# Two segments to a scan, states joined by hand, C products two ring slots back, halos on ScalarE

## The reference, cut to what matters

```python
u, gate = jnp.split(hidden_states @ W_in.T, 2, axis=-1)
u = silu(conv1d_causal(u, conv_w, taps=4) + conv_b)      # per channel
dt, Bm, Cm = split(u @ Wx.T);  dt, Bm, Cm = rmsnorm of each
delta = softplus(dt @ Wdt.T + dt_bias)                     # [L, D]
def step(state, xs):                                       # state [D, N]
    d_t, B_t, C_t, u_t = xs
    dA = jnp.exp(d_t[..., None] * A)
    state = dA * state + (d_t * u_t)[..., None] * B_t[:, None, :]
    return (state, jnp.einsum('bdn,bn->bd', state, C_t))
y = ys + u * D_param
return (y * silu(gate)) @ W_out.T
```

## Time and profile before

| what | us |
|---|---|
| median of 3 runs (1938.14 to 1943.71) | 1939.92 |
| the profiled execution | 1951.26 |
| its span | 1949.5 |
| VectorE busy in the span | 1376.4 |
| TensorE, matmuls | 1617.0 |
| ScalarE | 1094.3 |
| GpSimd | 1008.4 |

### The profile page before, as it was taken

How to read it: one execution, slowest core, us unless ns; L and a number is a source line. 1 busy time by engine, 2 the same in 40 slices (tenths; PEclk the granted TensorE clock), 3 DMA queues, 4 the chain that set the end, 5 groups by cost and what they waited for, 6 DMA issues and landing times. The chain is left out here.

```text
span 1949.5 us, 24260 instructions
## 1 busy us (share of the span) xinstructions
PE 1617.0 (83%) x8168; PEld 865.8 (44%) x8168; DVE 1376.4 (71%) x2292; ACT 1094.3 (56%) x2026; POOL 1008.4 (52%) x598
## 2 busy tenths in 40 slices
PE   6888999999779995788788797887978879745668
PEld 2522222222157443555365474654746547422322
DVE  3258888888073215038998899989999888999423
ACT  2334666667721113257766767668676676765127
POOL 0000000001033103447999899998999989999403
PEclk9866999999965796788698796997969879756678
DMA  5311000000083447543544455444554444545022
GB/s 225 154 52 56 3 3 3 3 3 3 7 297 145 149 129 262 185 107 76 117 103 99 105 123 114 103 98 106 122 115 103 99 104 110 118 98 123 19 91 87
DMA packets 152988, 195.78 MB, mean 100 GB/s; under 512 B 17907, under 2 KB 123139, under 8 KB 151198
## 3 DMA queue, kind: packets, MB, share of 16 engines
q1 hardware_dynamic: 143692, 167.19, 33.0%
q0 software_dynamic: 4608, 16.80, 2.4%
q10 hardware_dynamic: 4564, 10.24, 1.4%
HBM read 141.81 MB, written 52.37 MB: 100 GB/s over the span
## 5 line engine op out<-in xcount | busy, mean ns | idle before, releaser
L1810 DVE TENSOR_TENSOR_SCAN ssm_scan<-ssm_psum,ssm_state,ssm_scan 128x256 f32<-128x256 f32 x1024 | 680.2, 729 | 62.4 <-ACT ssm_psum L1697 61.2
L1429 POOL TENSOR_TENSOR ssm_scan<-ssm_scan,ssm_bc 128x1024 f32<-128x1024 f32 x256 | 554.1, 2176 | 78.3 <-DVE ssm_scan L1810 77.1
L1697 ACT ACTIVATE ssm_psum<-ssm_rep,ssm_a 128x256 f32<-128x256 f32 x1024 | 435.4, 468 | 190.6 <-DVE ssm_scan L1810 188.7
L641 ACT ACTIVATE att_probs<-att_psum 128x1024 f32<-128x1024 f32 x256 | 248.3, 1021 | 104.6 <-PE att_psum L577 104.3
L1409 POOL TENSOR_TENSOR ssm_scan<-ssm_rep,ssm_bc 128x1024 f32<-128x1024 f32 x128 | 301.5, 2356 | 9.2 <-DMA ssm_rep<-drive_rows 9.2
L678 DVE TENSOR_REDUCE att_rowmax<-att_psum 128x1 f32<-128x512 f32 x448 | 277.9, 682 | 38.1 <-PE att_psum L559 37.9
L1533 PE MATMUL ssm_psum<-ssm_scan,ssm_select 128*32 128x256 f32 x2048 | 192.3, 462 | 103.6 <-POOL ssm_scan L1429 103.3
L530 POOL COPY att_v<-v_tokens 128x128 f32<-128x128 f32 x8 | 2.3, 292 | 328.1 <-ACT att_out L635 328.1
L559 PE MATMUL att_psum<-att_k,att_q 72*128 72x512 bf16 x448 | 159.2, 395 | 3.7 <-DVE att_rowmax L678 2.2
L1795 DVE TENSOR_TENSOR ssm_scan<-ssm_rep,ssm_psum 128x1024 f32<-128x1024 f32 x128 | 156.2, 1220 | 1.1 <-DMA ssm_rep<-drive_rows 1.1
L1511 PE MATMUL ssm_psum<-ssm_h,late_weights 128*128 128x256 f32 x512 | 135.4, 424 | 18.2 <-DVE ssm_delta L1784 15.1
(11 more groups left out here) (232 smaller groups left out, 1892.2 us busy)
## 6 DMA issues: line engine op xcount, KB each, us to landing
ssm_rep<-drive_rows SPq DMA_DIRECT2D x256, 256.0 KB, 4.7
qkv_wmod<-in_wmod SPq DMA_DIRECT2D x8, 1536.0 KB, 11.9
late_weights<-in_we SPq DMA_DIRECT2D x8, 1024.0 KB, 14.3
ssm_bc<-bc_rows SPq DMA_DIRECT2D x32, 256.0 KB, 5.1
drive_rows<-ssm_delta SPq DMA_DIRECT2D x64, 128.0 KB
drive_rows<-ssm_du SPq DMA_DIRECT2D x64, 128.0 KB
sorted_rows<-moe_zeros SPq DMA_DIRECT2D x1, 5888.0 KB, 18.9
moe_sorted<-sorted_rows SPq DMA_DIRECT2D x23, 256.0 KB, 3.4
```

The source lines that it names most:

```text
L641: nc.scalar.activation(probs[:, u % RING, :].rearrange("p (j t) -> p j t", j=2), ps_s[u % 2], ACT.Exp).then_inc(exp_done, 1)
L1429: nc.gpsimd.tensor_tensor(read[:, Q % RING], drive[:, Q % RING], bc[:, c % 2, 1, gr, :].unsqueeze(1).to_broadcast([P, J, SW]), ALU.mult).t ...
L1697: nc.scalar.activation(ps_decay[n % HALF_BANKS][:, i], rep[:, s % 2, 0, j, :], ACT.Exp, scale=amat[:, t, gr, j:j + 1]).then_inc(decay_done, 1)
L1810: nc.vector.tensor_tensor_scan(drive[:, Q % RING, j, :], ps_decay[(2 * Q + j // 2) % HALF_BANKS][:, j % 2], drive[:, Q % RING, j, :], stat ...
```

## The change

A scan now covers two segments, 512 columns, with one instruction. The decay of the second segment's first column is set to zero once (`cut`, the decays of an odd segment then leave out their first column), so that the scan starts anew there. What the initial value did is done by hand: the first column's decay exp(A * delta) is computed for the tile (`first_decays`, two TENSOR_SCALARs of four columns on VectorE, and one Exp of eight columns on ScalarE), and `join` adds state times first decay to the first column of the drive for j = 1 and 3, two TENSOR_SCALARs of one column for each unit from chunk 1 on. Rows of the ring are 256 columns, dense; the product with C goes to the slot of two units before, so a spread waits for a sum two units closer; `bc` starts two columns later in memory. The halo copies go from VectorE to ScalarE, ahead of the copy of u. TensorE's and ScalarE's tables change: rows, square, the fourth output product and copy, Silu, the gate copies and the modulation of h move by one or two units.

```diff
+    PHASE = 2
-        halo = sb("ssm_halo", [P, DT, TAPS - 1])
+        halo = sb("ssm_halo", [P, 2, DT, TAPS - 1])
-        bc = sb("ssm_bc", [P, 2, 2, GROUPS, SW])
+        bc = sb("ssm_bc", [P, 2 * 2 * GROUPS * SW + PHASE])[:, PHASE:].rearrange("p (b s g t) -> p b s g t", b=2, s=2, g=GROUPS)
-        scan = sb("ssm_scan", [P, RING, J, SW + 1])
-        drive, read = scan[:, :, :, 1:], scan[:, :, :, 0:SW]
+        scan = sb("ssm_scan", [P, RING, J, SW])
+        first = sb("ssm_first_decay", [P, 2, GROUPS, J // 2])
-        U_COPY, CONV_OUT, GATE_OUT = {3: 0, 4: 1, 7: 2, 9: 3}, {6: 0, 8: 1, 10: 2, 12: 3}, {18: 0, 19: 1, 29: 2, 30: 3}
-        SILU, ROWS_OUT, RMS, GATE_SILU, H_OUT = 13, 16, 18, 31, 24
+        U_COPY, CONV_OUT, GATE_OUT = {2: 0, 4: 1, 7: 2, 9: 3}, {6: 0, 8: 1, 10: 2, 12: 3}, {19: 0, 20: 1, 29: 2, 31: 3}
+        SILU, ROWS_OUT, RMS, GATE_SILU, H_OUT = 12, 17, 18, 31, 22
-        OUT_COPY = {12: 0, 13: 1, 14: 2, 16: 3}
+        OUT_COPY = {12: 0, 13: 1, 14: 2, 15: 3}
+        def drive(Q):
+            return scan[:, Q % RING]
+        def read(Q):
+            return scan[:, (Q - 2) % RING]
...
-                if Q >= RING:
-                    pool.wait_ge(sum_done, Q - RING + 1)
+                if Q >= RING - 2:
+                    pool.wait_ge(sum_done, Q - RING + 3)
...
+                pair_of = slice(2 * pair, 2 * pair + 2)
+                nc.scalar.copy(upre[:, pair % 2, :, 0:TAPS - 1], halo[:, c % 2, pair_of, :])
+                nc.scalar.copy(halo[:, (c + 1) % 2, pair_of, :], halves("proj", c, pair)[:, :, SW - TAPS + 1:])
                 nc.scalar.copy(upre[:, pair % 2, :, TAPS - 1:], halves("proj", c, pair)).then_inc(upre_out, 1)
...
+                    if c >= 1:
+                        act.wait_ge(first_set, (s - DT + 1) * J // 2)
+                        nc.scalar.activation(first[:, s % 2], first[:, s % 2], ACT.Exp).then_inc(first_done, 1)
...
-                        nc.scalar.activation(ps_decay[n % HALF_BANKS][:, i], rep[:, s % 2, 0, j, :], ACT.Exp,
+                        nc.scalar.activation(ps_decay[n % HALF_BANKS][:, i, i:], rep[:, s % 2, 0, j, i:], ACT.Exp,
...
+            def first_decays(s):
+                c, t = s // DT, s % DT
+                dve.wait_ge(rep_in[s % 2], 64 * (s // 2 + 1))
+                if s >= DT + 2:
+                    dve.wait_ge(joined, (s - 1 - DT) * GROUPS * J // 2)
+                for j in range(1, J, 2):
+                    nc.vector.tensor_scalar(first[:, s % 2, :, j // 2], amat[:, t, :, j], rep[:, s % 2, 0, j, 0:1], None, ALU.mult).then_inc(first_set, 1)
+            def join(Q):
...
+                for j in range(1, J, 2):
+                    start = drive(Q)[:, j, 0:1]
+                    nc.vector.tensor_scalar(start, state[:, t, gr, j:j + 1], first[:, s % 2, gr, j // 2:j // 2 + 1], start, ALU.mult, ALU.add).then_inc(joined, 1)
...
+                for half in range(2):
+                    if half and not ON_DVE[q] and c >= 1:
+                        join(Q + 1)
+                    dve.wait_ge(decay_done, Q * J + 2 * half + 2)
+                    both = drive(Q)[:, 2 * half:2 * half + 2, :].rearrange("p j t -> p (j t)")
+                    nc.vector.tensor_tensor_scan(both, ps_decay[(2 * Q + half) % HALF_BANKS].rearrange("p j t -> p (j t)"), both,
+                                                 state[:, t, gr, 2 * half:2 * half + 1], ALU.mult, ALU.add).then_inc(scan_done, 2)
```

More of the change, by code:

```diff
@@ L1246, in state_space @@
         row_mm, row_out, wout_gated = sem("row_mm"), sem("row_out"), sem("wout_gated")
+        first_set, first_done, joined, cut = (sem(n) for n in "first_set first_done joined cut".split())
         gate_row = xout[:].rearrange("p k s -> p (k s)")[:, 0:D]
@@ L1254, in state_space @@
         xdst = scratch.x3.rearrange("(k p) t -> p k t", p=P)
[L1258 to L1261, removed]
+        AT = {0: [("proj", 0)],
+              1: [("proj", 1)],
+              3: [("conv", 0)],
+              4: [("proj", 2)],
+              6: [("conv", 1), ("proj", 3)],
+              7: [("conv", 2)],
+              9: [("conv", 3)],
+              10: [("out", 0)],
+              11: [("out", 1)],
+              12: [("out", 2)],
+              13: [("out", 3)],
+              15: [("rows", 0)],
+              16: [("square", 0)],
+              17: [("gate", 0)],
+              18: [("gate", 1)],
+              19: [("rms", 0)],
+              21: [("step", 0)],
+              22: [("step", 1)],
+              24: [("step", 2)],
+              25: [("step", 3)],
+              27: [("gate", 2)],
+              28: [("gate", 3)]}
         AHEAD = {"proj": 1, "conv": 1, "gate": 1, "rows": 1, "square": 1, "rms": 1, "step": 1, "out": -1}
@@ L1272, in at @@
             if q in AT:
-                kind, i = AT[q]
-                if 0 <= c + AHEAD[kind] < SCH:
-                    found.append((kind, c + AHEAD[kind], i))
+                for kind, i in AT[q]:
+                    of = c + (STEP_AHEAD[i] if kind == "step" else AHEAD[kind])
+                    if 0 <= of < SCH:
+                        found.append((kind, of, i))
             return found
@@ L1532, in sum_states @@
                 for j in range(J):
-                    last = nc.tensor.matmul(ps_y[t % 2][32 * j:32 * j + 32, :], select[:], read[:, Q % RING, j, :],
+                    last = nc.tensor.matmul(ps_y[t % 2][32 * j:32 * j + 32, :], select[:], read(Q)[:, j, :],
                                             start=(gr == 0), stop=False)
@@ L1704, in _ @@
             nc.scalar.copy(gate_row, psum[:, 7, :]).then_inc(row_out, 1)
+            act.wait_ge(zeroed, 1)
+            act.wait_ge(row_out, 1)
+            for bank7 in ps_decay:
+                nc.scalar.copy(bank7[:, 1, 0:1], state[:, 0, 0, 0:1]).then_inc(cut, 1)
             copy_u(0, 0)
@@ L1814, in unit @@
                     pair = slice((Q - 1) % RING, Q % RING + 1)
-                    nc.vector.tensor_reduce(state[:, t, gr - 1:gr + 1, :], scan[:, pair, :, SW:], AX.X, ALU.max).then_inc(carry_done, 1)
+                    nc.vector.tensor_reduce(state[:, t, gr - 1:gr + 1, :], scan[:, pair, :, SW - 1:], AX.X, ALU.max).then_inc(carry_done, 1)
             def gate_y(s):
@@ L1824, in _ @@
             dve.wait_ge(zeroed, 2)
-            for pair in range(DP):
-                carry_halo(0, pair)
-                save_halo(0, pair)
             dve.wait_ge(weights_in, 16 * 8)
@@ L1848, in _ @@
                         gate_y(c * DT + q // GROUPS - 1)
+                    s = c * DT + q // GROUPS
+                    if q % GROUPS == FIRST_DECAY and DT <= s + 1 < SCH * DT:
+                        first_decays(s + 1)
+                    if c >= 1 and not ON_DVE[q]:
+                        join(c * UNITS + q)
                     if c * UNITS + q + 1 < SCH * UNITS and ON_DVE[(q + 1) % UNITS]:
```

75 lines of the change are left out of this document (35 added, 40 removed).

## The result

The changed kernel takes 2055.91 us (median, 2052.43 to 2060.2) against 1941.82 in the same session, a ratio of 1.056 with a 95% interval of 1.053 to 1.060. Slower had been the likelier sign by little (0.47 against 0.45), and the time lies 51 us above the top of the range.

The account below looks back on a forecast made before the run. VectorE and GpSimd together were taken to bound the loop. A full chunk at 125.0 against 121.5 us gave +21 over six; with chunk 0 -9.5, the last +10.2 and start-up +1, +22.7, so 1963 us; range 1887 to 2005.

Parts of the forecast that it names:

- the likelier sign: Whole kernel: slower by more than about 0.3% had chance 0.47, faster 0.45, within 0.08.
- The hold: VectorE's first decays wait out GpSimd's product, eight times a chunk: 1.5 us each, 12 us a chunk.
- The feedback: State-space loop: with products at 2.12 us GpSimd is caught up at most scans, which makes the hold long.
- The joins: One-column multiply-adds on VectorE, 64 a chunk from chunk 1: 0.09 us each, 5.8 us a chunk (2.6 to 8.3).
- The merged scans: VectorE's scans of 512 columns follow after 1.20 us; a pair saves 0.10 us, 64 pairs 6.4 us a chunk.
- Together: Merge and joins in VectorE's work of a full chunk: -6.4 and +5.8 us.
- The order: Moved ScalarE and TensorE work cuts a full chunk's stalls from 10.9 to 4.5 us, 2.5 with the hold.
- GpSimd: Products and spreads go from 2.18 and 2.36 us to 2.12; GpSimd needs 105.5 us a chunk, from 111.3.
- rival 2: GpSimd gets no faster: 1919 us, or at 2.36 for both it bounds the loop, 1928 us; chance 0.20.
- The halos: Halo copies leave VectorE for ScalarE, 8 a chunk: 0.7 us a chunk off VectorE's work.
- Rival 1: The hold on VectorE's first decays costs nothing: a full chunk takes 115 us, the kernel 1890 us; chance 0.27.

Follow-up runs that it names:

- e1: The changed kernel with the first decays made by ScalarE alone, none on VectorE: 1925.48 us, ratio 0.988 to the kernel before.
- e4: The kernel of e1 with the joins left out, so the state is not carried into odd segments: 1892.08 us, ratio 0.970 to the kernel before.
- e2: The changed kernel with each four-column first decay cut into four of one column on VectorE: 1969.32 us, ratio 1.012 to the kernel before.
- e10: The changed kernel with four scans of 256 columns a unit again, no joins or first decays: 1908.55 us, ratio 0.978 to the kernel before.
- e13: The kernel of e10 with merged scans of 512 columns in chunk 0 alone, without joins: 1902.62 us, ratio 0.974 to the kernel before.
- e6: The kernel of e1 with bc at column 0 of its buffer instead of column 2: 1933.51 us, ratio 0.992 to the kernel before.
- e5: The kernel before with only the new order of the other work in a chunk: 1906.84 us, ratio 0.980 to the kernel before.

## Why the prediction was wrong

A full chunk went 121.5 -> 115.8 (all but the merge) -> 119.3 (merge and joins, nothing held) -> 137.2 us (the hold): -5.7, +3.5, +17.9. Point by point:

- **The hold: right in kind, mis-sized; this is the step that failed.** The mechanism, its place (0.07 us behind a product in the earlier trace rows, 0.04 now) and its eight times a chunk came true. The price was taken as 1.5 us for each tile, 12 a chunk, within 0 to 2.1. In the trace the 56 pairs hold VectorE 145.7 us, 2.60 each, 20.8 a chunk. That is (2.60 - 1.50) x 56 = 62 of the 93 us that the forecast was short; it alone takes 1963 to 2025, out of the range. The upper end was wrong by itself: it was one remaining product for the pair, but each of the two instructions waits for what GpSimd runs when that instruction comes up. After the product of the second group stands the multiply for `du`, 0.72 us, at every tile, and the second instruction waits for that too. That `du` stands there was to be read in the code. And the earlier trace rows said that the pair would start right behind a product, which is the whole product and not three quarters of it.
- **The feedback, in the direction the prediction gave.** With products of 2.00 us GpSimd has caught up before 239 of its 256 products (269 us idle on scans), so the product starts with the end of the unit's scans, and the pair behind them meets a fresh one.
- **The joins: mis-sized.** 0.09 us each was taken, 0.04 to 0.13. Two take 0.44 and one 0.26, so one follows another after 0.18: 64 x 0.18 = 11.5 us a chunk, not 5.8, above the range's end of 8.3. By busy time, e1 less e4, they cost 10.5, which is 7 x 4.7 = 33 us of the miss. The row they were costed by is one instruction of one column with another form; eight plain one-column TENSOR_SCALARs in e2 take 1.06 us, one 0.205, so 0.12 apart. A join has two pointers and a tensor that is read and written in place. Which of these makes the difference was not measured.
- **The merged scans: right.** Where one follows another directly in the changed kernel, the median from start to start is 1.19 us, for 1.20. Chunk 0 of e10 and e13 gives the saving: 6.4 us of VectorE's work for 64 pairs, 0.10 each, as forecast. In full chunks e10 and e4 differ by 109.5 - 103.7 = 5.7.
- **Together** merge and joins add 4.7 us to VectorE's work (114.2 in e1, 109.5 in e10), which is -5.7 + 10.5, where the prediction had -0.6. The full chunk grows by 3.5, since VectorE stands a microsecond less.
- **The order: right.** Stalls were to fall by 6.4 us a chunk without the hold; with the tables alone they fall by 5.4 and the chunk by 5.9. With the hold 2.5 us were to stay; 3.0 did.
- **GpSimd: right about the offset, of no weight.** 2.00 us for 2.12. By the rule of the Trainium skill, "GPSIMD Engine Reference", section Instruction dispatch, 2.13 was the estimated floor; the products measured here are quicker, and the measurement decides. The prediction feared a bound by GpSimd at 2.36 for both (rival 2, 120 us a chunk): e6 has that and takes 119.2 with VectorE's 114 us in it.
- **The halos**, which were not run alone, show no gain: VectorE's work went from 110.0 to 109.5 us a chunk between e5 and e10, and its idle time rose by a microsecond.
- **Rival 1 priced.** The kernel with no hold runs at 1925, not at 1890, because of the joins; the mean hold from which a full chunk loses was put at 1.1 us and is (121.5 - 119.3) / 8 = 0.3 us by these runs. 2.60 is past both.

With the hold at 2.60, the joins at 10.5 a chunk and the idle time at 3.0, the prediction's full chunk is 110.5 + 4.7 - 1.2 + 20.8 + 3.0 = 137.8 (the first decays' own 1.2 us is part of the 2.60; at the 0.09 that the prediction took, 16 of them are 1.4), and 137.2 was measured. The last chunk is 10.2 + 4.7 + 7 x 1.1 = 22.6 us longer than before, and 22.7 was measured. The terms are good to a microsecond or so, but none of the size of the hold or the joins is missing.

## What to carry to other kernels

Before putting a small SBUF to SBUF instruction on VectorE, look at what GpSimd starts at that moment: TENSOR_SCALARs of four and of five columns waited for the end of it here, once for every instruction (1.39 us in the mean), and the profile shows that as busy, not as a wait. Single columns (205 ns each) and ScalarE were ways round, and VectorE's spread, which reads B from PSUM, is not held beside the same kind of product: 1.22 us. When an instruction is merged, price the repair as carefully as the saving, by a row of the same form: here each merge saved 0.10 us and needed a join of 0.16 to 0.18. Measure a reordering by itself; here it was nearly the whole gain there was (ratio 0.980, where e13 reaches 0.974), and inside this change it could not be seen.

## What was not expected of the hardware

- **GpSimd's two-input operations depend on how its operands' starts lie to each other.** 1024 columns take 2.36 us where all rows start level, 2.00 with one or two columns between them, and the products 2.18 in the kernel before, with offsets of 1, 2, 3 and 4 columns, and again with -1, 0, 1 and 2. All are counted from the starts of the buffers; where these lie was not read. One reading, with 0.50 us a row when quick and 0.59 when slow, is that offsets of 1 and 2 are quick and those of 0, -1, 3 and 4 slow, which would be a period of four columns. Offsets of 3 and 4 by themselves were not run. Another reading is open: both kernels that show 2.18 have rows of 257 columns and write each product one column below where they read it, so that may set it instead. Their spreads, which write such rows too, do follow the offset (2.36 and 2.00).
- **A five-column instruction is held like a four-column one, a one-column one is not** (1385, 1386 and 205 ns).
- **A merged scan of 512 columns is 1.27 us long and follows the last after 1.19**, where two of 256 take 1.30: a merge saved 0.10 us, by the 6.4 us of 64 merges in e13's chunk 0.
